# Placing half of the edge records by target with TensorE's one-hots instead of GpSimd's scatter

## The reference

```python
# layer 0: two hops, weighted sums over edges grouped by one end
agg = segment_sum(val[:, None] * v[col], row, n)      # hop 0: once, hop 1: twice
y   = agg / safe_deg ; out = adaptive_enc(y, fc, bf)
# layer 1: attention over edges, softmax per group, messages summed
alpha = s_i[row] + s_j[col] + b_att ; ...softmax... ; segment_sum
# layer 2: transformer_conv, layer 3: message passing with layer norm
```

## Time and profile before

| what | us |
|---|---|
| median of three timed executions | 6757.92 |
| span of the profiled execution (first to last instruction) | 5289.8 |
| difference between the two | 1468.1 |
| GpSimd busy | 3461.7 |
| TensorE busy | 2873.2 |
| VectorE busy | 2794.9 |

### The profile page before, as it was taken

One profiled execution on the slowest core, in us unless ns is written; L12 is line 12 of the kernel. 1 busy time (PEld: TensorE's weight loads), 2 busy tenths in 40 slices (PEclk: granted clock), 3 DMA queues, 4 the chain that ended last, 5 costly groups with the idle time before them and its releaser, 6 DMA issues.

```text
span 5289.8 us, 73813 instructions
## 1 busy us (share of the span) xinstructions
PE 2873.2 (54%) x17389; PEld 2236.2 (42%) x17390; DVE 2794.9 (53%) x6391; ACT 791.8 (15%) x3180; POOL 3461.7 (65%) x3922
## 2 busy tenths in 40 slices
PE   5443477763333573034445877768986665643333
PEld 5333366653333463034443333356464333543333
DVE  8889822223221588033335988876147666971111
ACT  2121100000000100000001555456100001640000
POOL 3777677767777777777774777654047773017775
PEclk9999955555555555556556999878997766876566
DMA  2211222231112483033333444534169997732223
GB/s 62 67 29 47 68 52 52 52 46 26 27 27 25 60 115 47 18 69 79 81 81 59 137 127 127 133 91 139 40 191 316 335 331 221 268 124 52 52 52 53
DMA packets 303759, 526.16 MB, mean 99 GB/s; under 512 B 89450, under 2 KB 172640, under 8 KB 296928
## 3 DMA queue, kind: packets, MB, share of 16 engines
q1 hardware_dynamic: 177960, 289.53, 19.3%
q0 software_dynamic: 125728, 235.82, 18.3%
HBM read 423.29 MB, written 101.80 MB: 99 GB/s over the span
## 4 chain that ended last, share of the span: by engine, by line
POOL 42%; issue 28%; DVE 14%; PE 9%; DMA 2%; ACT 2%; DVEq 2%; POOLq 1%; SPq 1%; ACTq 0%; PEldq 0%
POOL work L789 31%; POOL rec_by_dst L749 6%; PE ps L2330 3%; POOL acc L789 2%; DVE acc L1568 2%; ACT work L1934 1%; DVE work L1027 1%; PE ps L2104 1%; POOL idx_slot L783 1%; PE ps L2045 1%; DVE work L1015 1%; PE ps L2401 1%; DVE work L973 1%; DVE work L1042 1%; DVE acc L1496 1%
## 5 line engine op out<-in xcount | busy, mean ns | idle before, releaser
L789 POOL DMA_INDIRECT work<-t_h,idx_slot x832 | 801.2, 963 | 546.2 <-DMA t_h<-acc 304.5
L2045 PE MATMUL ps<-work 128*128 128x128 f32 (+1 forms) x2496 | 700.0, 443 | 677.2 <-DMA work<-t_v,idx_slot 352.0
L789 POOL DMA_INDIRECT work<-t_v,idx_slot x832 | 789.2, 949 | 267.0 <-issue 221.9
L2045 PEld LDWEIGHTS ps<-work 128*128 128x128 f32 x2496 | 583.2, 328 | 700.5 <-issue 700.5
L789 POOL DMA_INDIRECT work<-t_xl,idx_slot x416 | 413.5, 994 | 123.8 <-issue 111.0
L2298 PE MATMUL ps<-big,work 128*128 x832 | 411.3, 647 | 105.7 <-DVE work L1246 68.9
L749 POOL DMA_INDIRECT rec_by_dst<-sc_rec_d,sc_idx x392 | 394.1, 1005 | 113.2 <-issue 104.6
L749 POOL DMA_INDIRECT rec_by_src<-sc_rec_s,sc_idx x392 | 388.6, 991 | 113.3 <-issue 104.2
L2370 PE MATMUL ps<-big,work 128*128 x832 | 326.4, 549 | 191.7 <-DVE aS L1630 153.5
L1102 DVE COPY relw<-rec_s 128x16 f32 x104 | 19.7, 189 | 672.8 <-PE ps L2045 672.2
L789 POOL DMA_INDIRECT work<-t_kv,idx_slot x208 | 201.3, 968 | 257.7 <-DMA t_kv<-big 173.1
(11 more groups left out here) (480 smaller groups left out, 6177.0 us busy)
## 6 DMA issues: line engine op xcount, KB each, us to landing
work<-rows_of_v_by_position SPq DMA_DIRECT2D x52, 1024.0 KB
work<-relT_by_dst SPq DMA_DIRECT2D x156, 256.0 KB
rows_of_h_by_position<-work SPq DMA_DIRECT2D x52, 512.0 KB
work<-rows_of_h_by_position SPq DMA_DIRECT2D x52, 512.0 KB
rows_of_v_by_position<-work SPq DMA_DIRECT2D x26, 1024.0 KB
rows_of_v_by_position<-acc SPq DMA_DIRECT2D x26, 1024.0 KB
work<-t_v,idx_slot POOLq DMA_INDIRECT x832
work<-relT_by_src SPq DMA_DIRECT2D x52, 256.0 KB
```

Source lines behind the costliest of these rows:

```text
L789: nc.gpsimd.indirect_dma_start(to, None, table, bass.IndirectOffsetOnAxis(ap=idx_slot[:, h * HU + k:h * HU + k + 1], axis=0)).then_inc(s_g ...
L2045: ins = M.matmul(psum_blocks[:, ds(b, 1), 0:width], oh[:, s, :], ring[:, h * HU + k, 0:width].unsqueeze(1), start=False, stop=False)
```

## The change

192 of the 392 columns are no longer scattered by GpSimd in the order by target. During the second hop of layer 0, in each of the 48 halves of rounds 1 to 12, VectorE makes for four of these columns two one-hots: one of the edge's row (128 by 128, from `place & 127`) and one of its tile (128 by 416, from `place >> 7`), the latter multiplied by the record, packed in one f32 number as `256 * source + row in the block + 1`. TensorE adds their product to one PSUM bank of 128 by 416 (bank 7, `records_sum`). After the hop VectorE copies the bank out, splits it with a shift and a mask, and adds it to the records that came back from the scatter, whose rows hold 0 and -1 where nothing was scattered. Since bank 7 is taken, the eight weighted one-hots of that hop read their iota from SBUF (`iota_f`).

The 200 other columns are scattered as before, 5 rounds instead of 9 or 10. `records_back(1)` moves ahead of the store of the softmax in SyncE's queue, and GpSimd waits for `rel_ready` instead of `s_rec` before layer 1's messages. Several semaphores are merged into counted ones (`degrees_summed`, `prefix` and `map_ready` into `sort_sums`, and others alike), one for one in the places where they stood.

```diff
+    PER_HALF = 4
+    MOVED = (G - 1) * 4 * PER_HALF
+    ROUNDS_BY_DST = (JE - MOVED) // (NS * HU)
+    FIRST_MOVED = JE - MOVED
...
-        SENT = [NG // NS - (h == NS - 1) for h in range(NS)]
+        SENT = [[NG // NS - (h == NS - 1), ROUNDS_BY_DST] for h in range(NS)]
...
             rel_rows("L1", 0)
+            records_back(1)
             sp.wait_ge(ph("scored"), SCORED["L1"])
             sp.dma_start(pos_dram.rearrange("(r x) f -> r (x f)", x=XR), shown[0:TQ, :, :].rearrange("p x f -> p (x f)")).then_inc(ph("pos_written"), 16)
-            records_back(1)
...
-            gate(s_rec, 32)
+            gate(ph("rel_ready"), 2)
...
+            def moved_edges():
+                at = slice(FIRST_MOVED, JE)
+                link(V.tensor_scalar(value_of, recE[1][:, at, 0].bitcast(i32), 256.0, 1.0, ALU.mult, ALU.add))
+                link(V.tensor_tensor(value_of, value_of, recE[1][:, at, 1], ALU.add))
+                link(V.tensor_single_scalar(whole, place_by_dst[:, at], 7, ALU.arith_shift_right))
+                link(V.tensor_copy(column_of, whole))
+                link(V.tensor_single_scalar(place_by_dst[:, at], place_by_dst[:, at], P - 1, ALU.bitwise_and))
+                link(V.tensor_copy(row_of, place_by_dst[:, at]))
+
+            def moved_one_hots(i, h):
+                for k in range(PER_HALF):
+                    n = (half_no(i, h) - S4) * PER_HALF + k
+                    edge = ds(n, 1)
+                    dve.wait_ge(ph("records_added"), n + 1)
+                    V.tensor_scalar(row_oh[:, k, :], iota_f[:, :], row_of[:, edge], None, ALU.is_equal)
+                    V.tensor_scalar(column_oh[:, k, :], iotaT, column_of[:, edge], value_of[:, edge],
+                                    ALU.is_equal, ALU.mult).then_inc(ph("moved_onehot"), 1)
+
+            def moved_records():
+                link(V.tensor_copy(moved_sum, records_sum))
+                link(V.tensor_single_scalar(moved_src, moved_sum, 8, ALU.arith_shift_right))
+                link(V.tensor_single_scalar(moved_sum, moved_sum, 255, ALU.bitwise_and))
+                link(V.tensor_copy(moved_rel, moved_sum))
...
-                            last = V.tensor_scalar(oh[:, h * HU + k, :], iota_p, pair[:, k, 0:1], pair[:, k, 1:2],
+                            last = V.tensor_scalar(oh[:, h * HU + k, :], iota_f[:, :] if name == "L0h2" else iota_p, pair[:, k, 0:1], pair[:, k, 1:2],
                                                    ALU.is_equal, ALU.mult)
                         last.then_inc(sig(name, "_onehot"), 1)
+                        if name == "L0h2" and not (isinstance(i, int) and i == 0):
+                            moved_one_hots(i, h)
...
+                if o == 1:
+                    source, row = rec[1][:, :, 0].bitcast(i32), rec[1][:, :, 1]
+                    link(V.tensor_tensor(source, source, moved_src, ALU.add))
+                    link(V.tensor_tensor(row, row, moved_rel, ALU.add))
...
+            def add_records(i, h):
+                for k in range(PER_HALF):
+                    pe.wait_ge(ph("moved_onehot"), (half_no(i, h) - S4) * PER_HALF + k + 1)
+                    M.matmul(records_sum, row_oh[:, k, :], column_oh[:, k, :], start=False, stop=False).then_inc(ph("records_added"), 1)
```

More of the change, by code:

```diff
@@ L222, in gnn_stack @@
         dhiF = h2T[:, 512:512 + T]
+        place_by_dst = bigf[:, 0:J].bitcast(i32)
+        column_oh = view(bigf, J, [PER_HALF, T])
+        row_oh = view(bigf, J + PER_HALF * T, [PER_HALF, P])
+        m0 = J + PER_HALF * (T + P)
+        row_of, column_of, value_of = (bigf[:, m0 + n * MOVED:m0 + (n + 1) * MOVED] for n in range(3))
+        whole = row_of.bitcast(i32)
+        assert m0 + 3 * MOVED <= 9 * J
+        moved_sum = bigf[:, 10 * J:10 * J + T].bitcast(i32)
+        moved_src, moved_rel = bigf[:, 10 * J + T:10 * J + 2 * T].bitcast(i32), bigf[:, 10 * J:10 * J + T]
+        assert 2 * T <= 3 * J
         def tile_innermost(s):
@@ L399, in gnn_stack @@
         SORTED = {"keys_ready": 1, "degrees": 2, "bases": 3, "ends": 4}
-        SENT = [NG // NS - (h == NS - 1) for h in range(NS)]
-        VALUES = [2 * SENT[g] * HU * 16 + CB * 16 for g in range(NS)]
+        SUMMED = {"degrees": 1, "prefix": 2, "map": 3}
+        SENT = [[NG // NS - (h == NS - 1), ROUNDS_BY_DST] for h in range(NS)]
+        VALUES = [sum(SENT[g]) * HU * 16 + CB * 16 for g in range(NS)]
         assert NS == CH
@@ L472, in each_half, with but_first @@
                     half(i, h)
+        def but_first(eng, half):
+            for h in range(S4):
+                half(0, h)
+            with eng.Fori(1, G) as i:
+                for h in range(S4):
+                    half(i, h)
         def ahead(eng, first, then):
@@ L758, in group @@
                     send(h, range(QU, HU))
-                last = NG // NS - 1
+                last = max(SENT[h][o] for h in range(NS)) - 1
+                final = sum(SENT[h][o] > last for h in range(NS))
                 slots(0, 0, o == 1)
@@ L766, in scatter @@
                         group(i, h, (i, h + 1) if h < NS - 1 else (i + 1, 0), True)
-                for h in range(NS - 1):
-                    group(last, h, (last, h + 1) if h < NS - 2 else None, True)
+                for h in range(final):
+                    group(last, h, (last, h + 1) if h < final - 1 else None, True)
                 for h in range(NS):
-                    gate(s_sc[h], (o + 1) * SENT[h] * HU * 16)
+                    gate(s_sc[h], sum(SENT[h][0:o + 1]) * HU * 16)
                 pool.sem_inc(s_scd, 1)
@@ L1977, in count @@
                 M.matmul(ps[:, 6, 0:NB], lower, deg[o][:, :], start=True, stop=True)
-                M.matmul(ps[:, 7, 0:NB], ones, deg[o][:, :], start=True, stop=True).then_inc(ph("prefix"), 1)
+                M.matmul(ps[:, 7, 0:NB], ones, deg[o][:, :], start=True, stop=True).then_inc(ph("sort_sums"), 1)
             def find(o):
@@ L2015, in find @@
                 pe.wait_ge(ph("sort_steps"), SORTED["ends"] + o * 4)
-                M.matmul(ps[:, 7, 0:T], ones[0:NB, :], flagT[0:NB, :], start=True, stop=True).then_inc(ph("map_ready"), 1)
+                M.matmul(ps[:, 7, 0:T], ones[0:NB, :], flagT[0:NB, :], start=True, stop=True).then_inc(ph("sort_sums"), 1)
             def open_sums(banks, zero_b=zero_b):
```

60 lines of the change are left out of this document (36 added, 24 removed).

## The result

The changed kernel took 6560.31 us (median of four runs, 6552.88 to 6572.94) beside 6759.53 us for the kernel before: a ratio of 0.972 with a 95% interval of 0.9693 to 0.9746, 199 us less. Two more sessions gave 0.972 (0.9677 to 0.9763) and 0.9694 (0.9664 to 0.9723). The prediction was 6680: the sign was right, the size was not, 199 us against 78.

What follows compares the result with a forecast made beforehand. GpSimd was taken as the bound, its scatter by target ending last. 108.2 - 26 - 5.6 - 1.9 + 3 = 77.7 us less gave 6680 us, own range 6645 to 6715, with rivals 6505 to 6728.

Steps and rivals of the forecast that it cites:

- I take them as standing around the execution, the same before and after: Timed median against profiled span: the 1468.1 us between them lie outside the execution, so 77.7 us come off 6757.9.
- Rival (3): Whole kernel: the 1468 us are inside, spread throughout (6659) or in the indirect DMAs, 0.444 us each (6506); chance 0.30.
- The scatter ends last, but by far less than its own length: Scatter by target against the softmax store: of 258 us of GpSimd's time removed, only 108.2 us can be had.
- Rival (4): Scatter by target: it isn't what ended last and its removal is worth nothing; no chance of its own.
- What that does to GpSimd: Second hop, layer 0: VectorE's SBUF operations delay GpSimd's DMAs, 0.55 us a half, 26 us in all (bounds 0 and 92).
- Rival (1): Second hop: VectorE's operations lock GpSimd out for their whole duration, 213 us instead of 26, so 6867; chance 0.06.
- What is added to TensorE: Second hop: 192 f32 matmuls of 416 columns at 1.4 us, a half 10.3 us against GpSimd's 10.65, barely hidden.
- rival (2): Second hop: TensorE becomes the bound, halves of 11.1 to 12.1 us, sums closing 20 to 70 us later; chance 0.14.
- VectorE's prices: One-hots in the hop: 0.23 us for 128 columns, 0.42 for 416, a half 4.6 us against 10.1, not the bound.
- Not hidden are the last half's four: End of the hop: four matmuls between the last gathered rows and the closing of the sums, 5.6 us (2.8 to 6.4).
- The 1.9 us for taking the sum apart: After the hop on VectorE: a copy from PSUM, two integer operations and a cast, with gaps, add 1.9 us.
- layer 1's chain without a scatter beside it: Layer 1's scores: their last 100 us run without a scatter beside them, 3 us off (bounds 0 and 12).

Runs made afterwards that it cites:

- the first trace: The kernel before, unchanged, in its first profiled execution, a short one: span 5289.8 us, while the timed executions took 6758.
- the addition alone: The changed kernel with all 392 columns scattered again; the sum of the 192 placed ones is made but left unused: 6794.22 us, 1.0052 of the kernel before.
- the iota alone: The kernel before with only the weighted one-hots of layer 0's second hop reading their iota from SBUF instead of PSUM: 6763.16 us, 1.0007.
- six: The changed kernel with six columns placed in each half instead of four (288 placed, 104 scattered): 6422.67 us, 0.9608 of the kernel before.
- eight a half: The changed kernel with eight columns placed in each half instead of four (384 placed, 8 scattered): 6394.09 us, 0.9479 of the kernel before.
- after_again: The changed kernel, unchanged, run once more in a later session: 6560.92 us, 0.972 of the kernel before.
- after_third: The changed kernel, unchanged, run once more in a further session: 6553.36 us, 0.9694 of the kernel before.
- after_look: The changed kernel, unchanged, one look in the last session: 6522.9 us in one run, beside 6714.43 for the kernel before.
- the removal alone: The changed kernel without the hop's placing one-hots and matmuls, so the 192 columns are neither scattered nor placed: 6542.27 us, 0.9677 of the kernel before.

## Why the prediction was wrong, point by point

**The step that failed** is the one between the sum and the time: "I take them as standing around the execution, the same before and after". They lie inside (span 6771.0 of 6772.68 us), and they change what ends the stretch. Rival (3) had the place right, and its range held the time, but its mechanism was wrong: it put the time into the indirect DMAs themselves, 0.444 us on each. They take 0.98 us in the long execution's scatter against 1.00 in the first trace, and the column 1.40 us against 1.345. In this stage it is what runs beside them that takes longer: the chain up to the store, 851.8 us instead of 411.1. The forecast's range held the time (6505 to 6728), but by rival (3)'s share alone; the mechanism that came out stood in no rival.

**"The scatter ends last, but by far less than its own length": 108.2 us.** For a short execution this is shown (113 us without the DMAs). In the long ones it is false: GpSimd waits 312.7 us for the softmax. The sum's first term is there not a wait that goes, but 267 to 272 us of scatter (549.9 less 283 or 278.0) times 0.77 to 0.84, 206 to 229 us, by which the chain is freed. Rival (4) had its condition fulfilled and its conclusion wrong: not last, and yet worth 220 us.

**"What that does to GpSimd": 26 us, and "halves of 10.5 to 10.8".** Against 0.55 us a half forecast, a half grew by 0.3 (11.6 to 11.9) and the hop by 14.7 us. GpSimd's own DMAs took 0.961 us instead of 0.953, so 0.06 us a half of it is theirs. With its copies GpSimd is busy 5.5 us longer in the hop, and its waits for TensorE's products grew by 9 us (74 to 83); whether TensorE's matmuls or VectorE's one-hots make those later was not separated. Rival (1) is out by the addition alone (36 us, not 213) and by the iota alone (0).

**"What is added to TensorE": 1.4 us a matmul, hidden barely.** The matmuls of 416 columns keep TensorE busy for 1.20 us each on average (220.5/184; a record of one of its two instructions lasts 743 ns, but the records overlap), and a pair by itself at the clock of 0.50 takes 1.76. The granted clock of the hop rose from 0.50 to 0.64, and with six and eight a half to 0.74 and 0.82. But the reading of who waits for whom was that of a short execution: in the long one GpSimd waits for TensorE in 13 of the 52 halves already before the change and in 22 after it, so rival (2)'s condition is met in part, at 9 us and not 20 to 70. TensorE's own wait for rows falls from 231.2 us to 44.7. Even eight cost only 0.8 to 0.9 us a half more than four. These groups are the changed kernel's, in the hop:

```profile
L814 POOL DMA_INDIRECT work<-t_v,idx_slot x416 | 400.0, 961 | 227.5 <-issue 117.1 <-remote 74.6 <-DMA t_v<-acc 27.3
L2125 PE MATMUL ps<-big 128*128 128x416 f32 x368 | 220.5, 743 | 173.7 <-issue 90.2 <-DVE big L1138 83.5
...
L1158 DVE TENSOR_SCALAR work<-iota_f,relw 128x128 f32<-128x128 f32 x408 | 110.6, 358 | 1.8
L1138 DVE TENSOR_SCALAR big<-big 128x416 f32<-128x416 f32 x184 | 92.2, 501 | 0.3 <-issue 0.3
...
L1137 DVE TENSOR_SCALAR big<-iota_f,big 128x128 f32<-128x128 f32 x184 | 57.2, 311 | 326.0 <-remote 262.4 <-PE ps L2125 56.5 <-issue 6.8
```

**VectorE's prices.** I took 0.23 and 0.42 us for the one-hots; they take 0.31 and 0.50, and a train of eight weighted ones 8 x 0.27 (110.6/408). A half is 0.3 + 2.2 + 3.2 = 5.7 us, under half of its 11.9.

**"Not hidden are the last half's four": 5.6 us.** In the long execution they are dear in another way: the last halves run into the scatter. The changed kernel's last four one-hots of a row and the end of the sums, on VectorE:

```profile
2348.15 0.53 DVE L1137 TENSOR_SCALAR big<-iota_f,big 128x128 f32<-128x128 f32 x1 [37.64 <-remote]
...
2354.45 0.28 DVE L1137 TENSOR_SCALAR big<-iota_f,big 128x128 f32<-128x128 f32 x1 [5.55 <-remote]
...
2360.04 0.34 DVE L1137 TENSOR_SCALAR big<-iota_f,big 128x128 f32<-128x128 f32 x1 [4.90 <-remote]
...
2365.65 0.28 DVE L1137 TENSOR_SCALAR big<-iota_f,big 128x128 f32<-128x128 f32 x1 [4.92 <-remote]
...
2446.78 0.59 DVE L1143 CAST big<-ps 128x416 int32<-128x416 f32 x1 [80.41 <-remote]
2447.41 0.38 DVE L1144 TENSOR_SCALAR big<-big 128x416 int32<-128x416 int32 x1
2447.82 0.42 DVE L1145 TENSOR_SCALAR big<-big 128x416 int32<-128x416 int32 x1
2448.28 0.38 DVE L1146 CAST big<-big 128x416 f32<-128x416 int32 x1
2448.69 0.19 DVE L1222 TENSOR_SCALAR work<-ps 128x25 f32<-128x25 f32 x1
```

The first of the last four waits 37.6 us and the sum 80.4 us, where nothing but TensorE's tail lies between. The sum is taken 151 us after the last gather (2295.55 to 2446.78), against 10 us in the kernel before (2288.11 to 2298.11). This trace is the mild one: in after_again, after_third, after_look and add_only the sum is taken 250 us after the last gather, where the removal alone is at that point after 70. At the store it comes to 6 us in this trace (622.6 against 616.8) and to 27 to 29 us in the three others, out of the 37 to 39 that placing costs there up to the store. So most of its price lies behind the hop and not in the 48 halves; that it is this tail is argued from the 250 us against 70. No kernel that leaves the last halves without placed columns was run. **The 1.9 us for taking the sum apart** came out as 1.91.

**Smaller terms.** For layer 1's chain without a scatter beside it I took 3 us off (0 to 12): in the short execution without any of its DMAs it took 402.4 us instead of 411.1. The reads start 12 us after the store instead of 10, and that nothing changes from the first read on was forecast and found (3619 and 3621 us).

## What to carry to other kernels

Hold the span of the profiled execution against the timed runs before anything else. Where they differ by a fifth, the profile is of another kind of execution, and its waits may end in another order; get a trace whose span equals its time before working out a gain from it. And an engine that waits for nothing can still hold others back by what it issues: its instructions are then worth removing from beside the critical chain even where it is idle at the end.

## What the runs showed of the hardware

- The same program takes 5290 to 5295 us or 6666 to 6787 us, the two on one chip. What decides between them was not found. In the long executions TensorE starts its instructions 0.70 or 1.40 us apart while GpSimd issues indirect DMAs, and its register operations take 0.70 us instead of 0.05. In the hop this sets in 23 to 34 us after GpSimd starts, in nine cases of ten, and is over 3 to 6 us after it stops.
- The rows of each DMA don't count there: 64 instead of 128 moved the store by 6 us of 852. Fewer DMAs do: 104 instead of 392 moved it by 306. Whether a GpSimd that is busy without DMAs holds TensorE back too stayed open.
- 416 gathers that fetch one and the same row for the edges left out take 705 us instead of 626, with the DMA engines busy 0.92 of the time instead of 0.31.
- The Trainium skill (SBUF — State Buffer, Who interferes with whom) would have VectorE's two-port operations lock GpSimd out for their whole length. Whether the one-hots ran in such a mode no row shows. With their iota in SBUF 52 x 8 of them cost nothing in the time (1.0007, 0.9988 to 1.0026); GpSimd's DMAs that begin during one take 0.968 us (median of 89) instead of 0.944. Longer ones cost more: in the first trace those that begin during the attention layers' comparisons of 1024 bf16 columns (line 1246, 0.5 us each) take 1.15 us (median of 89).
